# One exponential over both score banks of an attention step (1024 columns) in place of two over 512 columns each, in a two-layer Perceiver kernel

## The reference, cut to what matters

```python
qh = _split_heads(q @ Wq.T); kh = _split_heads(k @ Wk.T); vh = _split_heads(v @ Wv.T)
scores = jnp.einsum('bhqd,bhkd->bhqk', qh, kh) * scale       # scale = 1/sqrt(16)
attn = jax.nn.softmax(scores, axis=-1)                       # over 1601 context rows
out = jnp.einsum('bhqk,bhkd->bhqd', attn, vh)
...
x = x + _L0_xattn_ref(_layernorm(x), ctx_1024, ctx_1024, ...)
x = x + _L1_xattn_ref(_layernorm(x), ctx_1024, ctx_1024, ...)
```

## Time and profile before

| | |
|---|---|
| median of 3 runs | 1217.04 us (1215.41 to 1219.43) |
| the profiled execution: its own time, its span | 1223.86 us, 1222.1 us |
| PE busy | 1054.0 us, 86% of the span |
| DVE busy | 609.1 us, 50% |
| ACT busy | 548.9 us, 45% |
| POOL busy | 148.2 us, 12% |
| cross-attention steps (two layers, 8 batches, 13 steps) | 208 |

### The profile page before, as it was taken

One profiled execution on the slowest core, in us unless ns is written; L12 is line 12 of the kernel. 1 busy time (PEld: TensorE's weight loads), 2 busy tenths in 40 slices (PEclk: granted clock), 3 DMA queues, 4 the chain that ended last, 5 costly groups with the idle time before them and its releaser, 6 DMA issues.

```text
span 1222.1 us, 32026 instructions
## 1 busy us (share of the span) xinstructions
PE 1054.0 (86%) x13348; PEld 677.6 (55%) x13348; DVE 609.1 (50%) x869; ACT 548.9 (45%) x948; POOL 148.2 (12%) x167
## 2 busy tenths in 40 slices
PE   4799979999986968669999999988636899999998
PEld 2366646666664852236665666656414544444887
DVE  5655545556422335366564556562266754445432
ACT  5276666677660213426556565644005622221210
POOL 3211121112101000221212121210000000000000
PEclk9799999999996668879999999998656999999999
DMA  7844652563423200155343434320002122222210
GB/s 237 254 123 149 190 150 59 174 180 107 120 74 155 35 1 1 38 131 136 97 110 79 125 100 110 90 63 3 4 32 108 69 104 74 99 104 104 83 56 18
DMA packets 51376, 120.55 MB, mean 99 GB/s; under 512 B 16772, under 2 KB 26148, under 8 KB 47908
## 3 DMA queue, kind: packets, MB, share of 16 engines
q1 hardware_dynamic: 49768, 111.91, 32.0%
q0 software_dynamic: 1328, 6.54, 1.4%
q10 hardware_dynamic: 144, 0.07, 0.0%
HBM read 62.88 MB, written 16.26 MB: 65 GB/s over the span
## 4 chain that ended last, share of the span: by engine, by line
PE 47%; DVE 8%; ACT 3%; issue 1%; POOL 0%; DVEq 0%; ACTq 0%
PE ps L530 46%; DVE mpart L1182 2%; PE ps L821 1%; DVE rinv L1171 1%; ACT p L939 1%; DVE wl L1397 1%; DVE xcl L1445 0%; PE ps L681 0%; ACT wh L1051 0%; DVE v L1163 0%; DVE xc L1436 0%; DVE oT L1174 0%; ACT xch L1083 0%; DVE st_ssm L1117 0%; ACT kh L917 0%
## 5 line engine op out<-in xcount | busy, mean ns | idle before, releaser
L1182 DVE TENSOR_REDUCE mpart<-ps 128x2 f32<-128x800 f32 (+1 forms) x256 | 251.4, 990 | 175.0 <-PE ps L530 175.0
L939 ACT ACTIVATE p<-ps 128x512 f32<-128x512 f32 (+1 forms) x416 | 225.5, 594 | 132.7 <-PE ps L530 129.8
L482 POOL TENSOR_TENSOR kl<-k,kh 128x400 f16<-128x400 f32 (+1 forms) x128 | 121.5, 949 | 510.3 <-ACT kh L917 509.0
L530 PE MATMUL ps<-qcur,ks 97*128 97x128 f16 (+1 forms) x1664 | 134.5, 222 | 2.8 <-ACT p L939 1.1
L530 PE MATMUL ps<-p,v 128*17 128x64 f32 x6656 | 133.9, 222 | 0.7 <-issue 0.7
L530 PE MATMUL ps<-kh,qbcur 32*128 32x400 f16 (+1 forms) x512 | 90.2, 353 | 41.4 <-DVE mpart L1182 17.4
L530 PE MATMUL ps<-wvh,ch 128*128 128x256 f16 (+1 forms) x416 | 116.3, 279 | 9.2 <-issue 8.5
L530 PEld LDWEIGHTS ps<-p,v 128*17 128x17 f32 x6656 | 98.4, 98 | 37.8 <-issue 32.9
L1397 DVE SCALAR_TENSOR_TENSOR wl<-w,wh 128x2048 f16<-128x2048 f32 x24 | 55.0, 2292 | 125.7 <-ACT wh L1051 125.7
L530 PE MATMUL ps<-wvh,cl 128*128 128x256 f16 (+1 forms) x416 | 115.6, 278 | 0.0
L530 PE MATMUL ps<-wvl,ch 128*128 128x256 f16 (+1 forms) x416 | 115.5, 278 | 0.0
(11 more groups left out here) (222 smaller groups left out, 1445.3 us busy)
## 6 DMA issues: line engine op xcount, KB each, us to landing
ks<-kh SPq DMA_DIRECT2D x256, 100.1 KB
w<-in_wgu SPq DMA_DIRECT2D x16, 1024.0 KB, 4.8
ks<-kl SPq DMA_DIRECT2D x128, 100.1 KB
w<-in_wd SPq DMA_DIRECT2D x8, 1024.0 KB, 4.8
c<-in_ctxT SPq DMA_DIRECT2D x8, 801.0 KB, 5.1
cparts<-ch SPq DMA_DIRECT2D x8, 800.5 KB, 9.7
cparts<-cl SPq DMA_DIRECT2D x8, 800.5 KB, 11.2
c<-in_ctxT SPq DMA_DIRECT2D x8, 800.0 KB, 7.6
```

The lines of the kernel that those rows point to most:

```text
L482: nc.gpsimd.tensor_tensor(kl[:, mt, k0:k0 + w], k32[:, ku % 4, 0:w], kh[:, mt, k0:k0 + w], ALU.subtract).then_inc(sem("klo_done"), 1)
L530: return nc.tensor.matmul(o, lhsT, rhs, start=start, stop=stop, skip_group_check=shared)
L939: nc.scalar.activation(p32[0:n, exp_buffer(u, k), BANK * hb:BANK * hb + BANK], ps[0:n, hb, :], ACT.Exp, scale=DH ** -0.5).then_inc(sem("ex ...
L1182: nc.vector.reduce_max(mpart[:, j0:j0 + 2, quarter], o.rearrange("p (b c) -> p b c", b=2)[:, :, 0:w], AX.X).then_inc(sem("max_done"), 1)
```

## The change

Before, a step's scores were handed over bank by bank: the exponential of bank 0 could begin when its four matmuls had ended, and the first four matmuls of the next step waited only for the exponential of bank 0, the other four for that of bank 1. Now one ACTIVATE reads both banks through `flat`, a flat view of the same memory, and writes the same 1024 columns of `p32`. It waits for all eight matmuls; exp_done counts one per step; and all eight matmuls of the next step stand behind the whole exponential. What is computed stays the same.

```diff
                 for hb in range(2):
-                    need(pe, "exp_done", 2 * KT * g + 2 * k - 1 + hb)
+                    if hb == 0:
+                        need(pe, "exp_done", KT * g + k)
                     for jj in range(4):
...
-                pe.wait_ge(sem("exp_done"), 2 * KT * g + 2 * k + 2)
+                pe.wait_ge(sem("exp_done"), KT * g + k + 1)
...
                 need(act, "pv_mm", KT * g + k - steps_back(exp_buffer, u, k) + 1)
-                for hb in range(2):
-                    act.wait_ge(sem("main_mm"), 2 * KT * g + 2 * k + hb + 1)
-                    nc.scalar.activation(p32[0:n, exp_buffer(u, k), BANK * hb:BANK * hb + BANK], ps[0:n, hb, :],
-                                         ACT.Exp, scale=DH ** -0.5).then_inc(sem("exp_done"), 1)
+                act.wait_ge(sem("main_mm"), 2 * KT * g + 2 * k + 2)
+                nc.scalar.activation(p32[0:n, exp_buffer(u, k), :], flat[0:n, 0:2 * BANK], ACT.Exp,
+                                     scale=DH ** -0.5).then_inc(sem("exp_done"), 1)
```

## The result

The changed kernel took 1237.12 us (median of 4 runs, 1234.3 to 1238.63) beside 1218.24 us for the kernel before (4 runs, 1215.41 to 1223.56): a ratio of 1.0147, with a 95% interval of 1.0105 to 1.0189. It is slower, as forecast, but 1237 lies above the forecast's own range of 1227 to 1234, and also above 1236, up to which the forecast went for its rivals. Each ratio is the recorded estimate with its interval and not the quotient of the two medians, from which it differs by up to 0.2%.

The account below looks back on a forecast made before the run. PE was taken to bound the kernel, with ACT mattering only where PE waits for it. Delays of 5.4 + 7.1 + 0.5 + 0.4 = 13.4 us on a median of 1217.04 gave 1230 us, range 1227 to 1234.

Parts of the forecast that it names:

- Later start and later hand-back: Between one step's scores and the next: at least 1.74 us in the loop's batches, 1.79 in those written out.
- (a): Steps 0 to 1 in the 14 batches not last of a layer: 0.39 us later each, 5.4 us in all.
- (b): Steps 5 to 12 of the two last batches: 3.55 us longer each, 7.1 us in all.
- (d): Steps 10 to 11 of layer 0's next-to-last batch: 0.4 us later; layer 1's costed at nothing.
- (c): Steps 0 to 1 of the two last batches: 0.25 us in layer 1, the same taken for layer 0, 0.5 in all.
- The wait taken away is worth nothing: Each step's score matmuls lose their second wait; it has no visible price where it doesn't stall, so no gain.
- Waits: Expected sign in the profile: PE's waits for exponentials rise from 9.1 us to about 20.
- Only the last batches pay: Rival: in middle batches the step 1 delay vanishes in PE's other waits; 8.0 us left, 1225 us; chance 0.12.
- The relief of ACT wins: Rival: ACT sets the pace, so 0.06 us saved at 208 steps brings 12.5 us: 1204.5 us; chance 0.03.
- The clock falls in the last batches: Rival: emptier last batches drop to 1.2 GHz, 3.1 us more in each: 1233 with one, 1237 with both; chance 0.13.
- No difference: Rival: something outside PE's order paces the layers and 13 us of PE's delay are hidden: 1217 us; chance 0.06.
- the toss of the clock: Layer 1's next-to-last batch, up to 3.3 us gained or lost in either layer by a mere shift of work; widened the range.

Follow-up runs that it names:

- late_start: Kernel before, two exponentials and hand-back bank by bank kept, but the first starts only when all eight matmuls have ended: 1232.6 us, ratio 1.0095.
- whole_wait: Kernel before, two exponentials started bank by bank, but the next step's score matmuls wait for both: 1230.0 us, ratio 1.0062.
- last_split: Changed kernel with two exponentials again in the last batch of each layer only: 1226.82 us, ratio 1.0044 against the kernel before.
- last_merged: Kernel before with one merged exponential in the last batch of each layer only: 1229.85 us, ratio 1.0067.
- covered_merged: Changed kernel with two exponentials at steps 0 and 10 and in the whole last batches: 1219.55 us, ratio 0.9986 against the kernel before.
- after_again: The changed kernel run again without edit, 6 runs against 29 of the kernel before: 1234.12 us, ratio 1.0122.
- both comparisons: The changed kernel against the kernel before, measured twice: ratio 1.0147 with 4 runs, then 1.0122 with 6 runs.
- after_v2: Changed kernel with step 0 ordered P0, S, V2, W in place of V2, P0, S, W: 1232.12 us, ratio 1.0083 against the kernel before.
- before_p0: Kernel before with step 0 ordered V2, S, P0, W in place of V2, P0, S, W: 1217.48 us, ratio 0.9968.

## Why the prediction was right in its mechanism and wrong in its time

- *What bounds the kernel.* Right: the time was lost on PE, at the places where only W stands between two S.
- *The instruction.* Right: 1024 ns, 1.02 us was taken; 208 of them have a busy sum of 212.8 us, 212 was forecast.
- *Later start and later hand-back.* Right: 1.74 and 1.80 us from S to S against 1.74 and 1.79. late_start and whole_wait show that the waits do it and not the instruction.
- *(a) and (b).* Right: 0.39 us in a middle batch (0.37 in the windows above), 1.80 us per step in the last ones. last_split leaves (a) and (d), 6.4 us at equal clock for 5.8; last_merged leaves (b) and (c), 6.7 for 7.6.
- *(c).* In layer 1 the last batch began at half clock before and at full clock after, so the 0.25 us can't be read there. Layer 0's began at full clock in both: from the first load of step 0 to the end of the last one of step 1 it takes 2.17 us before (343.35 to 345.52) and 2.34 after (349.55 to 351.89), 0.17.
- *(d).* Right: from S to S 1.43 us before and 1.79 after (340.63 to 342.42), 0.36 for 0.4.
- *The wait taken away is worth nothing.* Nothing contradicts it; it was not tried by itself.
- *Waits.* About 20 us was forecast for PE's waits for exponentials. PE's matmuls wait 19.0 us, at 31 places, the number that the forecast had counted. Its weight loads wait 31.2 us at 59 places. Of these, 24.3 us belong to the loads of scores (a matmul's wait of 0.61 us stands as 0.71 to 0.78 in its load's row), and the other 6.9 us, at 28 places, to the loads of W. The same places idle as long in the kernel before, put down to issue there, and the idle time before W's loads did not rise in all (36.5 us, 37.8 before), so these 6.9 us cost nothing:

```profile
PE ps L530 <- ACT p L939: 19.0, 31, 1.2
L530 PEld LDWEIGHTS ps<-qcur,ks 97*128 97x128 f16 (+1 forms) x1664 | 96.2, 99 | 43.0 <-ACT p L939 24.3
```

W in the same batch, the kernel before, then the changed one:

```profile
661.30 0.47 PEld L530 LDWEIGHTS ps<-p,v 128*17 128x17 f32 x32 [0.33 <-issue]
670.67 0.47 PEld L530 LDWEIGHTS ps<-p,v 128*17 128x17 f32 x32 [0.33 <-ACT p L939]
```

- *Rivals.* Only the last batches pay: fell by last_split, whose interval excludes 1. The relief of ACT wins: fell by covered_merged. The clock falls in the last batches: it didn't in the profile after, nor in that of after_again; where it was below full in layer 1's last batch of last_merged (0.95), it was so in the kernel before as well (0.94). No difference: fell by both comparisons.

**The step that failed** is "the median of the runs is 6.8 us lower, and 1217.04 + 13.4 gives 1230", with the range "1227 to 1234" laid around it. The term that was mis-sized is 1217.04; the 13.4 us measured 13.1 at equal clock. The forecast took three runs as the level of the kernel before. On three chips its medians are 1221.5 us (29 runs), 1222.69 us (23) and 1221.85 us (24), and single runs go from 1215.19 to 1227.84. From 1221.5 the same sum gives 1234.9, and ten runs of the changed kernel, both comparisons together, lie between 1230.3 and 1243.45 with a mean of 1236.1. The profiled execution of before, at 1223.86, was not an odd one 6.8 us too slow, as I took it, but 2.4 us above the 1221.5, where the median of the three is 4.5 below. That is 4.5 of the 7.1 us between 1230 and the 1237.12 measured first. Of the rest most is clock: those four runs spent 207.5 us at half clock on average, where the 29 of before spent 200.9, and at 0.36 that is 2.3 us.

In the first comparison itself the base was not far off, for its four runs of before, which include the three, have a median of 1218.24: the same low sample stood on one side, and a sample with more half clock than usual on the other, hence 18.9 us between the two medians. Both intervals (12.8 to 23 and 9.5 to 20 us) hold 13.4, and the estimate at equal clock leaves room for no more than about 1.5 us above it. The forecast named the cause, the toss of the clock, at 3.3 us in one batch, and sized it too small. Over a whole execution it is worth some 12 us from the fastest to the slowest. The 3.3 us itself compared layer 1's batch with layer 0's; the same batch at full clock takes 37.40 us (covered_merged), so half clock had cost 2.7 there. What sets the clock's toss from one execution to the next, no run here shows.

## What to carry to other kernels

Merging two instructions over two banks saves 0.06 us on their own engine here (1.08 us for the pair, 1.02 for the one), and gives up both overlaps with the producer: the early start and the early hand-back. Count, for every place where the producer comes back to the same banks, how much of its own work lies in between; where that is less than start + instruction + hand-back (1.8 us here), keep the split or give it a second set of banks; elsewhere it made no difference here (covered_merged). Where work is moved to cover a wait, look at what else the moved work waits for (after_v2), and at what the other engine does first (layer 0 of before_p0). Before adding a difference to a time, ask how many executions that time rests on and how the granted clock varied over them: three runs within 4 us of each other came from a spread of 12.

## What the runs showed of the hardware that was not expected

The granted clock differs between executions of the same kernel on one chip, with the time following it (0.923 and 1216.01 us, 0.911 and 1227.5 us; 0.36 us for each us more at half clock over 76 runs). It is at its two levels, 1.2 and 2.4 GHz, at different places each time. Layer 1's next-to-last batch, where the planned work is thin, is the clearest: 40.06 us at a mean clock of 0.90 in the profile before, 37.79 at 1.00 in that of the changed kernel, where PE waits longer at steps 0 to 1. So a longer wait in a batch did not mean a lower clock in it.
